# A second expert layer on tiles of 128 tokens, with resident weights and routed rows that carry the address of their result

## What is computed

```python
x = x + _L0_xattn_ref(_layernorm(x, axis=-1), ctx_512, ...)
x = x + _L0_ffn_ref(_layernorm(x, axis=-1), ...)
x = x + _L1_xattn_ref(_layernorm(x, axis=-1), ctx_512, ...)
x = x + _L1_ffn_ref(_layernorm(x, axis=-1), ...)

# the last one: 16 experts in 4 groups, width 176, two experts per token out of the two best groups
shared = silu(xf @ sw1[0]) @ sw2[0]
scores = sigmoid(xf @ gate_w.T)
# group score = sum of a group's two best; the other two groups are masked; top 2, weights normed to sum 1
out = shared
for e in range(16):
    out = out + combine[:, e:e + 1] * (silu(xf @ w1[e]) @ w2[e])
```

## Time and profile before

| | us |
|---|---|
| time, median of 3 runs | 2129.89 |
| lowest and highest | 2122.06 and 2139.57 |
| the profiled execution, as a run | 2129.46 |
| its span in the trace | 2127.6 |
| TensorE busy in the span | 1731.1 (81%) |
| VectorE, ScalarE, GpSimd busy | 1389.7, 842.1, 872.3 |

### The profile page before, as it was taken

One profiled execution on the slowest core, in us unless ns is written; L12 is line 12 of the kernel. 1 busy time (PEld: TensorE's weight loads), 2 busy tenths in 40 slices (PEclk: granted clock), 3 DMA queues, 4 the chain that ended last, 5 costly groups with the idle time before them and its releaser, 6 DMA issues. The chain is left out here.

```text
span 2127.6 us, 31873 instructions
## 1 busy us (share of the span) xinstructions
PE 1731.1 (81%) x9910; PEld 1202.2 (57%) x9910; DVE 1389.7 (65%) x2608; ACT 842.1 (40%) x2180; POOL 872.3 (41%) x762
## 2 busy tenths in 40 slices
PE   4999918999999999999999617999944899627870
PEld 3677604555555555555555417999933676527860
DVE  4677777777777777777775425777744566536663
ACT  2100003444444444444444215656612566316650
POOL 0466607777777777777755151000032000050005
PEclk9999957999999999999999858999975899758885
DMA  5533351222222222222100034555411000135654
GB/s 170 202 67 70 74 171 59 67 68 66 69 67 66 67 68 65 65 67 66 62 21 9 10 129 158 197 198 197 171 53 45 1 0 0 35 112 177 192 179 110
DMA packets 117869, 195.34 MB, mean 92 GB/s; under 512 B 49349, under 2 KB 95401, under 8 KB 112321
## 3 DMA queue, kind: packets, MB, share of 16 engines
q1 hardware_dynamic: 109569, 180.87, 27.1%
q0 software_dynamic: 8192, 13.15, 2.1%
HBM read 146.99 MB, written 46.63 MB: 91 GB/s over the span
## 5 line engine op out<-in xcount | busy, mean ns | idle before, releaser
L781 ACT ACTIVATE R<-banks 128x400 f32<-128x400 f32 x768 | 333.7, 505 | 341.4 <-PE banks L815 339.0
L591 DVE TENSOR_REDUCE PM<-banks 128x2 f32<-128x964 f32 x320 | 360.9, 1133 | 155.7 <-PE banks L568 154.0
L629 POOL TENSOR_TENSOR EA<-EA,R 128x400 f32<-128x400 f32 x288 | 313.4, 1088 | 177.6 <-ACT R L781 164.6
L815 PE MATMUL banks<-QS,KH 128*128 128x400 f32 x768 | 309.2, 403 | 2.4 <-DMA QB<-ML 1.5
L825 PE MATMUL banks<-R,KV 128*64 128x400 f32 x1536 | 299.9, 512 | 0.0
L815 PE MATMUL banks<-QB,KB 128*128 128x400 f32 x768 | 265.8, 346 | 0.0
L1314 POOL DMA_INDIRECT m_back<-rows_out,m_slots x64 | 65.0, 1016 | 464.0 <-DMA rows_out<-m_ys 434.9
L609 DVE TENSOR_TENSOR banks<-banks,R 128x400 f32<-128x400 f32 x320 | 183.9, 575 | 54.8 <-ACT R L781 54.1
L815 PEld LDWEIGHTS banks<-QS,KH 128*128 128x128 f32 x768 | 145.2, 189 | 108.5 <-ACT R L781 58.9
L1298 POOL DMA_INDIRECT rows_in<-m_XN,m_slots x64 | 65.5, 1023 | 339.9 <-POOLq L1017 267.5
L568 PE MATMUL banks<-KH,QS 64*128 64x482 f32 x320 | 160.7, 503 | 53.3 <-DVE KB L541 46.1
(11 more groups left out here) (248 smaller groups left out, 3627.9 us busy)
## 6 DMA issues: line engine op xcount, KB each, us to landing
m_stage_u<-in_m_up SPq DMA_DIRECT2D x20, 1392.0 KB
raw<-in_ctx_T SPq DMA_DIRECT2D x16, 1444.0 KB, 6.1
m_xg<-rows_in SPq DMA_DIRECT2D x55, 256.0 KB
rows_out<-m_ys SPq DMA_DIRECT2D x55, 256.0 KB, 6.1
m_stage_d<-in_m_down SPq DMA_DIRECT2D x20, 696.0 KB
QS<-queries SPq DMA_DIRECT2D x16, 800.0 KB, 6.8
rows_in<-zeros SPq DMA_DIRECT2D x5, 1792.0 KB
queries<-q_out_h SPq DMA_DIRECT2D x64, 100.0 KB, 2.4
```

The lines of the kernel that those rows point to most:

```text
L591: nc.vector.tensor_reduce(PM[:, 2 * i:2 * i + n], banks[:, k:k + n, 0:KW], AX.X, ALU.max).then_inc(red_done, 1)
L629: nc.gpsimd.tensor_tensor(out, first, tile_of(n, 1), ALU.add).then_inc(odd_sum, 1)
L781: nc.scalar.activation(tile_of(n, o), psum[S0 + (2 * n + o) % SB][:, 0:CH], ACT.Exp).then_inc(exp_done, 1)
L815: last = nc.tensor.matmul(out, lhs[r][:, keys], heads[:, o], start=lhs is KH, stop=lhs is KB)
```

## The change

The second expert layer leaves `moe` and `experts` and has its own code; the first one keeps the old path.

Tiles have 128 tokens (TOK1), so 40 tiles can be needed. The weights of all 16 experts and the shared one are loaded into SBUF as a whole (`GroupedWeights`, 3.06 MB each for up and down) by two transfers that SyncE issues in the layer norm block of the causal attention. The routed matmuls are plain float32 matmuls, with the rows as the stationary operand and the weights as the moving one; the up result is transposed again before the down matmul. The expert's number is read into TensorE's registers, 40 loads after the shared expert. The shared expert is computed densely from XH and XL, ahead of the tiles: its up matmuls as three float32r products, its down matmuls in float32, and VectorE adds the sums to X.

Each row in the list has a 257th value: the place of its result. `route` writes it beside the normalized row, in two copies of the rows (`tagged`), the second made by GpSimd in the routing block. The places are ROWS1 + n * 1600 + token for choice n. The DRAM list `tagged_rows` is cleared at the start of the kernel (with a smaller `rows_in`), so an empty row has place 0. VectorE takes the maximum of the place and the row's own slot number as an integer (`token`), and GpSimd scatters the 128 results of each tile into `results` by these numbers. So the results lie in the order of the tokens, and the gathers of before become 16 direct loads (`back`), each with both results of a sequence, into 16 buffers. The release of the semaphores ahead of the layer is gone, and its loops are written out.

```diff
+TOK1 = P
...
-def most_tiles(experts):
-
-    return (2 * B * S + experts * (TOK - 1)) // TOK
...
-ROWS = TOK * (-(-B * S // TOK) + most_tiles(E1))
+def most_tiles(experts, tok=TOK):
...
+    return (2 * B * S + experts * (tok - 1)) // tok
...
+ROWS = TOK * most_tiles(E0)
+ROWS1 = TOK1 * most_tiles(E1, TOK1)
+DW1 = D + 1
...
-                for r in range(0, ROWS // P, 14):
-                    sp.dma_start(rows_in[r * P:(r + 14) * P].rearrange("(p j) d -> p j d", p=P), zeros[:]).then_inc(cleared, 16)
+                for r in range(0, ROWS // P, 10):
+                    sp.dma_start(rows_in[r * P:(r + 10) * P].rearrange("(p j) d -> p j d", p=P), zeros[:, 0:10]).then_inc(cleared, 16)
+                tagged = tagged_rows.rearrange("(p j) d -> p (j d)", p=P)
+                for r in range(0, tagged.shape[1], CLEAR):
+                    sp.dma_start(tagged[:, r:r + CLEAR], zeros[:].rearrange("p j d -> p (j d)")[:, 0:CLEAR]).then_inc(cleared, 16)
...
-            @block.sync
-            def _(sp):
-                stores(sp)
...
+                if tagged is not None:
+                    for b in range(B):
+                        nc.gpsimd.tensor_copy(tagged[:, 1, b, 0:D], tagged[:, 0, b, 0:D]).then_inc(copied, 1)
+                    pool.wait_ge(copied, B)
...
                 vec.tensor_tensor(WL[:, :, 0:E], inputs.router[:], as_f32(WH[:, :, 0:E]), ALU.subtract).then_inc(parts, 1)
+                vec.tensor_scalar(steps[:], inputs.order[:, 0:FULL], float(tok), None, ALU.mult)
+                vec.tensor_copy(order[:, 0:min(tiles, LISTED)], inputs.order[:, 0:min(tiles, LISTED)])
+                if tiles > LISTED:
+                    vec.tensor_scalar(order[:, LISTED:], inputs.order[:, 0:tiles - LISTED], float(LISTED), None, ALU.add)
+                if tagged is not None:
+                    do(vec.tensor_reduce(behind[:], tri[:], AX.X, ALU.add))
+                    do(vec.tensor_scalar(behind[:], behind[:], -1.0, float(ROWS1 + S - 1), ALU.mult, ALU.add))
+                    do(vec.tensor_scalar(tokens[:], inputs.order[:, 0:2 * B], float(S), None, ALU.mult))
+                    for n in range(2):
+                        do.apart(vec.tensor_scalar(tagged[:, n, :, D:],
...
-            inputs = RouterInputs(core, stage, dram, tag, E, tiles)
-            plain = core.sem(tag + "plain")
-
-            def plain_rows(sp):
-                if first_tile:
-                    sp.dma_start(rows_in[0:B * S].rearrange("(b s) d -> s b d", b=B), XN[:]).then_inc(plain, 16)
-                    sp.wait_ge(plain, 16)
...
+class GroupedWeights:
+
+
+    I, TR, NT = 176, 88, 2
...
+        sp.dma_start(self.up[:].rearrange("p e k i -> p e (k i)"),
+                     self.dram["m1_up"].rearrange("e p k n i -> p e (k n i)")).then_inc(self.loaded, 16)
+        sp.dma_start(self.down[:].rearrange("p e t d -> p e (t d)"),
+                     self.dram["m1_down"].rearrange("e p t d -> p e (t d)")).then_inc(self.loaded, 16)
...
+    tag, tiles = "m1_", most_tiles(E1, TOK1)
+    with ExitStack() as ctx:
+        tagged = fixed(ctx, nc, tag + "tagged", [S, 2, B, DW1])
+        XN = tagged[:, 0, :, 0:D]
...
+        with ExitStack() as stage:
+            inputs = RouterInputs(core, stage, dram, tag, E1)
+            layernorm(core, tag + "ln_", X, XN, ident, XH, XL, B - 1, inputs.load)
+            route(core, inputs, tag, ident, XH, XL, E1, slots, w, tile_expert, tiles, TOK1, True, tagged)
+        grouped_experts(core, X, tagged, XH, XL, ident, slots, w, tile_expert, tagged_rows, results, weights, tiles, out)
...
+    UW, DW, I, TR, NT = weights.up, weights.down, weights.I, weights.TR, weights.NT
+    BUFS, RING = 4, B
+    UP, XB, HB, TB, YB = 0, 0, 2, 4, 6
...
+            @block.sync
+            def _(sp):
+                def load(k):
+                    if k >= BUFS:
+                        sp.wait_ge(turned, k - BUFS + 1)
+                        sp.wait_ge(token_ready, k - BUFS + 1)
+                    sp.dma_start(xg[:, k % BUFS, :], tagged_rows[k * TOK1:(k + 1) * TOK1]).then_inc(x_in[k % BUFS], 16)
+
+                sp.wait_ge(scattered, 16 * 2 * B)
+                for k in range(BUFS - 1):
+                    load(k)
+                for k in range(tiles):
+                    if k + BUFS - 1 < tiles:
+                        load(k + BUFS - 1)
+                for u in range(BUFS):
+                    sp.wait_ge(stored[u], 16 * len(range(u, tiles, BUFS)))
+                for b in range(B):
+                    sp.dma_start(back[:, b], results[ROWS1:].rearrange("(n b s) d -> b s n d", n=2, b=B)[b]).then_inc(back_in[b], 16)
+                for b in range(B):
+                    sp.wait_ge(added, b + 1)
+                    sp.dma_start(out[b], X[:, b, :]).then_inc(written, 16)
+                sp.wait_ge(written, 16 * B)
+
+            @block.gpsimd
+            def _(pool):
+                nc.gpsimd.iota(slot[:], [[P, tiles]], base=0, channel_multiplier=1,
+                               allow_small_or_imprecise_dtypes=True).then_inc(numbered, 1)
+                for b in range(B):
+                    for n in range(2):
+                        pool.indirect_dma_start(tagged_rows[:, :], bass.IndirectOffsetOnAxis(slots[:, n, b:b + 1], 0),
+                                                tagged[:, n, b, :], None).then_inc(scattered, 16)
+                for k in range(tiles):
+                    pool.wait_ge(y_done, k + 1)
+                    pool.wait_ge(token_ready, k + 1)
+                    pool.indirect_dma_start(results[:, :], bass.IndirectOffsetOnAxis(token[:, k % BUFS, :], 0),
+                                            ys[:, k % BUFS, :], None).then_inc(stored[k % BUFS], 16)
+
+            @block.tensor
+            def _(pe):
+                pe.wait_ge(weights.loaded, 32)
+                pe.wait_ge(split_lo, KD)
+                for n in range(NU):
+                    c, t = divmod(n, NT)
+                    if n >= 4:
+                        pe.wait_ge(s_hid, n - 3)
+                    cols, part = slice(c * CH, (c + 1) * CH), slice(t * TR, (t + 1) * TR)
+                    split_products(nc, psum[UP + n % 4][0:TR, 0:CH],
+                                   [(SH[:, q, part], SL[:, q, part], XH[:, q, cols], XL[:, q, cols])
+                                    for q in range(KD)]).then_inc(s_up, 1)
+                for m in range(PAIRS):
+                    pe.wait_ge(s_hid, NT * (2 * m // CB + 1))
+                    if m >= 2:
+                        pe.wait_ge(s_added, m - 1)
+                    for j in range(2):
+                        b = 2 * m + j
+                        for t in range(NT):
+                            last = nc.tensor.matmul(psum[YB + m % 2][0:S, j * D:(j + 1) * D], hidden[:, t, b * S:(b + 1) * S],
+                                                    DW[:, E1, t, :], start=t == 0 and j == 0, stop=t == NT - 1 and j == 1)
+                    last.then_inc(s_down, 1)
+
+                def turn(k):
+                    pe.wait_ge(x_in[k % BUFS], 16 * (k // BUFS + 1))
+                    if k >= 2:
+                        pe.wait_ge(xt_ready, k - 1)
+                    for q in range(KD):
+                        last = nc.tensor.transpose(psum[XB + k % 2][:, q * P:(q + 1) * P], xg[:, k % BUFS, q * P:(q + 1) * P],
+                                                   ident[:, :])
+                    last.then_inc(turned, 1)
+
+                def expert_of(k):
...
+
+                def up(k, e):
+                    pe.wait_ge(xt_ready, k + 1)
+                    if k >= 2:
+                        pe.wait_ge(hid_ready, k - 1)
+                    for q in range(KD):
+                        last = nc.tensor.matmul(psum[HB + k % 2][:, 0:I], xt[:, k % 2, q, :],
+                                                UW[:, e, q, :].rearrange("p o i -> p (o i)"), start=q == 0, stop=q == KD - 1)
+                    last.then_inc(up_ready, 1)
+
+                def turn_hidden(k):
+                    pe.wait_ge(hid_ready, k + 1)
+                    if k >= 2:
...
+                def down(k, e):
+                    pe.wait_ge(ht_ready, k + 1)
+                    if k >= 2:
+                        pe.wait_ge(y_done, k - 1)
+                    for t in range(NT):
+                        last = nc.tensor.matmul(psum[YB + k % 2][:, 0:D], ht[:, k % 2, t, :],
+                                                DW[:, e, t, :].rearrange("p o d -> p (o d)"), start=t == 0, stop=t == NT - 1)
+                    last.then_inc(down_done, 1)
+
+                e_of = [expert_of(k) for k in range(tiles)]
+                pe.wait_ge(s_hid, NU)
+                pe.wait_ge(s_added, PAIRS)
+                turn(0)
+                for k in range(tiles + 2):
+                    if k + 1 < tiles:
+                        turn(k + 1)
+                    if k < tiles:
+                        up(k, e_of[k])
+                    if 1 <= k <= tiles:
```

(87 more changed lines are left out.)

119 lines of the change are left out of this document (93 added, 26 removed).

## The result

The changed kernel takes 2119.05 us (2115.98 to 2128.88) against 2129.48 for the kernel before. The ratio is 0.9952, interval 0.9938 to 0.9967: half a per cent faster, inside the 1% that the prediction called no change. The forecast was 24.9 us less, 10.4 came. The trace of the changed kernel spans 2118.3 us.

A forecast was written before the change was run, and what follows sets the result against it. Loop bound by transfers and TensorE together, then an end without matmuls. Start 1925.5, first result 7, 36 turns 131.4, last three 6.8, end 31.2 reach 2101.9; small terms and span-to-run difference give 2105 us, range 2090 to 2134.

The forecast's parts named there:

- Start of the loop: Before the first routed tile: scatters bring rows at 1924.2, TensorE is ready at 1925.2; taken as 1925.5, bounds 1924 and 1941.
- warm 13.8 in all. From 1878.9 ... that ends at 1903.2: Shared expert on TensorE before the loop: its 32 down matmuls take 13.8 us, and the whole ends at 1903.2.
- The tie of the two paths: At the loop's start, scattered rows (1924.2) and TensorE's matmuls with register reads (1925.2) were to be ready nearly together.
- Their sum of 24.5: TensorE's 40 register loads after the shared expert, 0.61 us each, 24.5 us in all.
- Bound B's 1941: Late start of the tile loop: register loads at 1.0 us each put it at 1941, the time at 2120.
- The pace: Tile loop: VectorE's list waits for the scatter of tile k-3 to land (2.67 us); 36 turns of 3.65 us, 131.4.
- Rival C: Tile loop: the scatter lands later, 3.4 us, giving a turn of 4.38 us and 2131 us; chance 0.19.
- The end: After the loop: 16 loads, adds hidden beneath, then the output stores, 31.2 us to 2101.9; bounds 29 and 35.
- 19.9 for the load: At the end: the 16 loads of results, 3.28 MB at 165 GB/s, take 19.9 us.
- rival E: At the end: loads use all engines, some 260 GB/s, 8 us less, 2097 us and below; chance 0.07.
- The rest: GpSimd copies in routing 1 us, attention weight loads up to 5, clearing at most 3, removed release gains 1.
- rival B: Late loop start (1941, time 2120) or 1.2 GHz array; with that start, 1% slower from a 4.6 us turn; chance 0.14.

The follow-up runs named there:

- e3: The changed kernel, with GpSimd waiting for all sums of the shared expert before its 32 scatters: 2114.27 us.
- a0: The changed kernel unaltered, run again in a later series as control: 2089.67 us against 2114.29 for the kernel before, ratio 0.9898.
- e2: The changed kernel with eight buffers in place of four for the list of places and the results: 2061.38 us, ratio 0.9693 to the kernel before.
- e6: The changed kernel plus 64 rounds of TensorE transpose, ScalarE copy and VectorE copy between the shared expert's up and down matmuls, beside the scatters: 2185.62 us.
- series 1 and 2: First two sets of follow-up runs, each on one chip beside the kernel before, which took 2129.6 and 2128.1 us.
- series 3 to 5: Last three sets of follow-up runs, each on one chip beside the kernel before, which took 2113.2, 2114.3 and 2115.0 us.
- e5: The changed kernel with a PSUM bank for each of the eight pairs of shared down sums: 2117.45 us, ratio 0.9944 to the kernel before.
- e8: The changed kernel with the 64-round chain of e6 beside 32 added scatters of 64 values per row, not 257; full scatters follow: 2172.01 us.

## Why the prediction was right and wrong

**Start of the loop: wrong by 30.4 us, and it decides.** The step that failed is "warm 13.8 in all. From 1878.9 ... that ends at 1903.2". The size of the work was right (14.0 in e3), its neighbour was left out: it took the pitch from undisturbed rows and laid it beside 32 scatters. It ended at 1937.4, 34 us late; about 7 of these are the clock of the last 32 instructions, the rest is hold-up. The tie of the two paths, on which the reads' price of nothing rested, was then gone. Their sum of 24.5 was nearly right: they take 26.1 us, of which 19.7 stick out behind the shared expert, and 26.4 in a0. The 2.5 us by which they begin ahead of the last matmul's end stand in no row of the prediction; a0 shows just that, and at 1.2 GHz it is 5.9. Bound B's 1941 priced the reads too high and had no case for a late shared expert. The hint was in the trace: with the scatter of the earlier trace rows beside it TensorE was busy for 14.32 of 48.10 us in that stretch of the earlier trace rows, and ScalarE waited 5.75 and 11.21 us for nothing named. I read those as the start of a pipeline.

**The pace: right in mechanism, 0.43 us too long.** The wait stands where it was put, once for each of 36 tiles, and e2 shows it. The landing is 2.43 us, not 2.67, and 128 rows cost GpSimd 0.97, no more than 100. 31 turns take 3.2 us and five 3.8 to 5.2 us, which the sum had no term for: 7 us more than 36 short ones. So 8.4 us less in all is partly two errors against each other. By the Trainium skill (DMA: Bandwidth & Descriptors, Anatomy of one DMA) 2.0 us and 0.3 for the bytes make 2.3, near the measured 2.43; my mistake in that sentence was to add GpSimd's 1.0, which that time already holds. Rival C has no case.

**The end: 7.6 us too long.** The term "19.9 for the load" was mis-sized: it took 165 GB/s for the loads and 190 for the stores from the earlier trace rows, and both move 227 to 239 at 0.67 of the engines. That is rival E's size without its reason, for the share of the engines is that of the earlier trace rows; why they move more at the same share stays open. The adds, taken as hidden, very nearly were not.

**The rest** held, but for a slip in rival B, where a turn of 4.5 and not 4.6 gives 1% slower: the block starts 1.2 us later, the 16 copies take 5.6 us of GpSimd and hold nobody, the weight loads cost nothing that shows.

**Where the expected gain went**: 30.4 us to the start, 16.0 of it paid back by turn and end. In the series without hold-up the difference is 24.6 us against 24.9 forecast, but this is two errors that cancel: the sum is 14 us too long, and the kernel before is 15 us quicker there.

## What to carry to other kernels

Work that is put beside a dense row of GpSimd scatters is not always free (28 us here in one set of runs, nothing in another): read first how the engine fared beside such scatters in the trace at hand, and treat a wait with no named releaser there as a price. When a step is costed at nothing because another hides it, write down how late the cover may come; here 20 us of reads surfaced so. And where a ring of buffers is as deep as the lag in the code, one transfer's landing becomes the turn; four more buffers of 1 KB a partition were worth 54 us.

## What the hardware showed that I had not expected

TensorE was held up beside GpSimd's scatters 1.3 us apart, with no common data (the chain of e6 works on a constant): 2.21 us for what takes 0.51. Beside scatters 2.42 us apart it was not. It was so in both traces of the first comparison and in series 1 and 2, and never in series 3 to 5, at the same GB/s. The chip numbered 0 stands on both sides, in series 2 and 5. What decides, and what in TensorE waits, is not settled. One trait may help whoever looks further: the late starts in e5 lie 1.4, 2.1, 2.8 and 3.5 us apart, whole multiples of 0.70 us to within 0.02, and the long rounds of e6 are 2.1 and 2.8. The Trainium skill (SBUF — State Buffer, Who interferes with whom) says that TensorE and ScalarE never wait on anyone at the SBUF, and that a VectorE copy can wait for GpSimd. The second shows in e6 and e8: beside the scatters VectorE's copy takes 0.41 to 0.43 us in most rounds of 1.3 us, after them 0.23 in rounds of 1.1. In the long rounds of e6 it takes 0.23 too but for one, so this is not the hold-up; the runs do not place TensorE's hold-up at the SBUF, so they do not refute the first, but a reader of it alone would have left this cost out, as I did.

Recorded starts of matmuls can run ahead of the work: in e5 41 of them stand before 1894.7, and the signal behind the 24th reached VectorE at 1913.9. And the landing of a scatter is longer in four to six of the 36 turns, by 0.3 to 2.2 us, mostly seven to nine turns apart, in every trace of the loop with four buffers.
